# Eight 128x2048 sums of a float32 kernel, made by GpSimd instead of VectorE

## What is computed

```
x = x + W0[i015[b]] applied over the 64 rows          (L0, 64x64 per batch)
x = x + W1[i015[b]] applied over the 64 rows          (L1, 64x64 per batch)
x = x + x W^T + 0.5 (x A[i02[b]]) B^T                 (L2, W is 1024x1024, rank 32)
x = x + x W3[i37[b]]^T                                (L3, one of 8 adapters, 1024x1024)
```

## Time and profile before

| | |
|---|---|
| runs | 382.86, 383.15, 383.18 us (median 383.15) |
| profiled execution, span | 381.9 us |
| TensorE busy, 1738 matmuls | 375.4 us, 98% |
| VectorE | 267.3 us, 70% |
| ScalarE | 224.6 us, 59% |
| GpSimd | 114.9 us, 30% |
| HBM traffic over the span | 159 GB/s |

### The profile page before, as it was taken

How to read it: one execution, slowest core, us unless ns; L and a number is a source line. 1 busy time by engine, 2 the same in 40 slices (tenths; PEclk the granted TensorE clock), 3 DMA queues, 4 the chain that set the end, 5 groups by cost and what they waited for, 6 DMA issues and landing times.

```text
span 381.9 us, 7677 instructions
## 1 busy us (share of the span) xinstructions
PE 375.4 (98%) x1738; PEld 311.7 (82%) x1739; DVE 267.3 (70%) x302; ACT 224.6 (59%) x299; POOL 114.9 (30%) x156
## 2 busy tenths in 40 slices
PE   8999999999999999999999999999999999999995
PEld 5788888888888888888888888888888888888884
DVE  2796978856849888538869367854599635999653
ACT  3589568496246476235465465853677536779443
POOL 0000140100000000024765347563167532676600
PEclk9999999999999999999999999999999999999999
DMA  7985904640368484415437316652256622565223
GB/s 259 399 303 186 366 0 165 218 162 9 111 228 281 151 312 140 165 45 203 144 99 251 86 23 192 206 168 58 57 173 218 167 58 58 200 203 155 60 64 85
DMA packets 24187, 61.38 MB, mean 161 GB/s; under 512 B 1906, under 2 KB 2098, under 8 KB 24114
## 3 DMA queue, kind: packets, MB, share of 16 engines
q1 hardware_dynamic: 23648, 60.10, 47.6%
q10 hardware_dynamic: 466, 0.44, 0.4%
HBM read 52.15 MB, written 8.39 MB: 159 GB/s over the span
## 4 chain that ended last, share of the span: by engine, by line
PE 96%; DMA 2%; SPq 1%; DVE 0%; issue 0%; ACT 0%
PE ps L1526 45%; PE ps L1382 12%; PE ps L1383 12%; PE ps L1384 12%; PE ps L1409 4%; PE ps L1552 4%; PE ps L1618 2%; PE ps L1421 2%; DMA ring_f<-wt 2%; PE ps L1448 2%; PE ps L1567 0%; PE ps L1458 0%; SPq L315 0%; PE ps L1651 0%; DVE ring L906 0%; SPq L321 0%
## 5 line engine op out<-in xcount | busy, mean ns | idle before, releaser
L1526 PE MATMUL ps<-ring,aT 128*128 x752 | 173.2, 389 | 0.0
L1526 PEld LDWEIGHTS ps<-ring,aT 128*128 128x128 f32 x752 | 141.1, 188 | 29.6 <-issue 0.3
L1382 PE MATMUL ps<-ring 128*128 128x512 f32 x208 | 81.1, 390 | 0.0
L1383 PE MATMUL ps<-ring 128*128 128x512 f32 x208 | 81.0, 389 | 0.0
L1384 PE MATMUL ps<-ring 128*128 128x512 f32 x208 | 80.9, 389 | 0.0
L481 POOL TENSOR_TENSOR aT<-xT,aT 128x512 fp32r<-128x512 f32 (+1 forms) x36 | 56.2, 1581 | 47.4 <-ACT aT L766 42.4
L1273 DVE TENSOR_TENSOR ring<-raw,ring 128x1024 f32 (+1 forms) x40 | 61.7, 1600 | 6.2 <-ACT ring L752 6.2
L772 ACT ACTIVATE aT<-ps 64x1024 fp32r<-64x1024 f32 x32 | 32.7, 1023 | 47.5 <-PE ps L1526 47.1
L1301 DVE TENSOR_TENSOR stage<-ps,stage 64x1024 f32<-64x1024 f32 x30 | 36.7, 1222 | 28.9 <-ACT stage L781 28.2
L1290 DVE TENSOR_TENSOR aT<-ps,aT 64x1024 fp32r<-64x1024 f32 x32 | 39.1, 1222 | 21.5 <-ACT aT L772 20.8
L1382 PEld LDWEIGHTS ps<-ring 128*128 128x128 f32 x208 | 39.1, 188 | 8.1
(11 more groups left out here) (98 smaller groups left out, 326.9 us busy)
## 6 DMA issues: line engine op xcount, KB each, us to landing
raw<-w3t SPq DMA_DIRECT2D x40, 512.0 KB, 4.4
ring_f<-xt SPq DMA_DIRECT2D x8, 1024.0 KB, 8.7
raw<-xt SPq DMA_DIRECT2D x8, 1024.0 KB, 5.3
out<-stage SPq DMA_DIRECT2D x30, 256.0 KB, 3.2
ring_f<-wt SPq DMA_DIRECT2D x4, 1024.0 KB, 8.1
xT<-xt SPq DMA_DIRECT2D x3, 1024.0 KB, 10.4
xT<-wt SPq DMA_DIRECT2D x2, 1024.0 KB, 15.9
ring_f<-wt SPq DMA_DIRECT2D x4, 256.0 KB, 5.4
```

What stands on the lines that cost most here:

```text
L1382: pe.matmul(dst, hi_of(qw)[:, k, cs], hi_of(qx)[:, k, :], start=start and k == 0, stop=False, skip_group_check=True)
L1383: pe.matmul(dst, hi_of(qw)[:, k, cs], lo_of(qx)[:, k, :], start=False, stop=False, skip_group_check=True)
L1526: last = pe.matmul(acc(i)[:, n, :], x3_split(i, k, start, P), ring[:, bass.ds(off + (part * D + n * 512), 512)], start=(k == 0 and j == 0) ...
```

## The change

The functions t3, t2, t4 and t1 move from VectorE's program to GpSimd's, unchanged but for the engine. They leave VectorE's list at eight places. In GpSimd's list T3(0) and T2(0) stand ahead of the S3 diagonals, T4(0) between the S3 and the A22 diagonals, and the other five behind the A22 diagonals. Three of them get a wait for VectorE's low parts (semaphore x_lo), which its own order gave before: T3(1) for x0 to x5, T2(1) for x0 to x6, T4(1) for x0 to x8.

```diff
--- before.py
+++ after.py
@@ -519,10 +519,55 @@
+            def t3(j):
+                pool.wait_ge(s("keep"), 16 * (j + 1))
+                pool.wait_ge(s("stg"), in_stg(f"B12_{j}"))
+                pool.tensor_tensor(keep, keep, stg, ALU.subtract).then_inc(s("T3"), 1)
+            def t2(j):
+                pool.wait_ge(s("T3"), j + 1)
+                if j == 0:
+                    pool.wait_ge(s("b11"), 16)
+                else:
+                    pool.wait_ge(s("stg"), in_stg("B11_1"))
+                pool.tensor_tensor(stg, stg if j else b11, keep, ALU.add).then_inc(s("T2"), 1)
+            def t4(j):
+                n = 6 + 3 * j
+                pool.wait_ge(s(f"x_in{n}"), 16)
+                pool.wait_ge(s("T2"), j + 1)
+                v = raw_of(x_slot(n))
+                pool.tensor_tensor(v, v, stg, ALU.subtract).then_inc(s("T4"), 1)
+            def t1(j):
+                pool.wait_ge(s("stg"), in_stg(f"B11_{j} again"))
+                if j == 0:
+                    pool.wait_ge(s("x_in10"), 16)
+                    v = raw_of(x_slot(10))
+                else:
+                    pool.wait_ge(s("kw"), 48)
+                    v = kw
+                pool.tensor_tensor(v, v, stg, ALU.subtract).then_inc(s("T1"), 1)
+            t3(0)
+            t2(0)
             pool.wait_ge(s("S3"), 1)
             w_eyes(w2t, "S3")
+            t4(0)
             pool.wait_ge(s("w_in4"), 16)
             w_eyes(raw_of(w_slot(4)), "A22")
+            pool.wait_ge(s("x_lo"), HALF * 6)
+            t3(1)
+            pool.wait_ge(s("x_lo"), HALF * 7)
+            t2(1)
+            pool.wait_ge(s("x_lo"), HALF * 9)
+            t4(1)
+            t1(0)
+            t1(1)
...
             s3()
-            t3(0)
-            t2(0)
             low_parts(1)
...
             mix_twice()
-            t4(0)
             x_los(6)
             w_los(4, raw_of(w_slot(4)))
-            t3(1)
-            t2(1)
             x_los(7, stg)
             x_los(8, keep)
             take(6)
-            t4(1)
             x_los(9)
             s1()
-            t1(0)
...
             c22(0)
-            t1(1)
             x_los(13, kw)
```

More of the change, by code:

```diff
@@ L924, in x_los @@
                     x_lo(n, src, ks)
[L926 to L958, removed]
             def s2():
```

## The result

The changed kernel takes 391.44 us (389.48 to 391.87, four executions) against 383.11 (382.86 to 383.18): ratio 1.021, 95% interval 1.0185 to 1.0235. It is slower, as forecast, but by 8.3 us and not by 4.3, and the time is above the range.

A forecast was written before the change was run, and what follows sets the result against it. TensorE's unbroken matmuls bound the kernel, so relieving VectorE gains nothing. New waits of 1.6 and 2.7 us sum to 4.3; with the 383.15 us median that gives 387.4, range 385.0 to 390.2 us.

The forecast's parts named there:

- What bounds the kernel: From 18 to 182 us TensorE's matmuls run without a break, so taking work off VectorE gains 0.
- One sum, 4.5 us: One 128x2048 sum on GpSimd takes 4.5 us, against 2.29 on VectorE; at most 5.1.
- Not slower: Rival: with sums below 3.6 us all is hidden and the time is 383.2 us; chance 8%.
- The turns: GpSimd and two-SBUF-input VectorE operations alternate, so a VectorE operation meeting a sum can lose up to 4.5 us.
- Only the chain: Rival: low_lows and T3(1) meet no waits, leaving 2.1 to 2.7 us at P6(1); 385.2 to 385.9 us; chance 15%.
- Step 1: T3(0) and T2(0): low_lows wait behind T2(0), so TensorE waits 1.6 us at C11(1)'s first delta.
- Step 2: Chain of sums and loads from T4(0) to x7: x7's half reaches P6(1) 2.7 us late.
- Where it would be waited for: Of the 2.7 us, some 2.4 at C21(0) for w4's second half and 0.3 at P6(1).
- The clock: TensorE's granted clock falling below 1.00 behind a wait: named as a sign of being wrong, given no size.
- Step 3: T4(1), T1(0) and T1(1) cost 0, with cover down to a few tenths of a us.

The follow-up runs named there:

- e4: The changed kernel with only T4(1), T1(0) and T1(1) on GpSimd, the other five sums back on VectorE; 382.95 us.
- e6: e1 and e2 together: six sums on GpSimd, T2(0) behind the low_lows, T3(1) and T2(1) on VectorE; 382.97 us.
- e1: The changed kernel with one added wait: T2(0) on GpSimd starts only when both low_lows of chunk 1 are done; 386.96 us.
- e10: e5 with 27 small extra matmuls on TensorE, meant to fill its wait at P6(1); 389.32 us.
- e3: The changed kernel with 30 small extra matmuls on TensorE ahead of P6(1), inside the wait; 389.97 us.
- e9: e1 with T4(0), T3(1), T2(1) and the loads between them in halves, plan steps as in e5, T3(1) behind w4's low parts; 384.97 us.
- e7: The changed kernel with T3(1) alone back on VectorE, behind w4's low parts; 386.80 us.
- e11: The changed kernel with 14 small extra matmuls on TensorE ahead of P6(1), to fill part of the wait; 391.95 us.
- e5: e1 with two portions of VectorE's plan steps moved from ahead of x6's low parts to behind x8's; 390.58 us.
- e2: The changed kernel with T3(1) and T2(1) back on VectorE, the other six sums on GpSimd; 385.51 us.

## Why the prediction was wrong

**What bounds the kernel**: right. e4 and e6 took 3 and 6 sums off VectorE and gained nothing.

**One sum, 4.5 us**: nearly right, 4.58 to 4.61 where nothing is met. The slope between the two widths held. *Not slower*, which needed under 3.6, falls.

**The turns**: right, for small operations too (5.10 us for low_lows, undone by e1), and too narrow. I read them as a matter of two SBUF inputs, but in e10 VectorE's two copies, which have one SBUF input, took 5.33 us together beside T4(0), in place of 0.87. *Only the chain* falls with it.

**Step 1, 1.6 us**: the wait was 1.5, and 0.3 came with it for the restart, which I had no term for.

**Step 2, 2.7 us**: this term was mis-sized. The wait was 3.8. From x6's landing to P6(1) I counted 26.7 us (70.5 to 97.2); it took 27.7 (71.8 to 99.5), against about 23.9 allowed. Of the 1.0, 0.2 is in the sums (4.6 each, while the 0.1 allowed for a turn in T4(0) wasn't used), 0.3 in T3(1)'s turn (5.52, so 0.9 in place of 0.6), and 0.5 in the hops between landing, sum, ScalarE, VectorE and TensorE, some 0.1 to 0.2 each, most of which I had left out.

**Where it would be waited for**: wrong for this kernel, right for e1. I had T3(1) between w4's halves; it came some 0.2 us after the second half had begun and waited for its end (82.64), as T4(0) began at 71.86, 0.15 us after the copies behind VectorE's plan steps had ended, and the A22 diagonals met nearly nothing. I had taken this as mere bookkeeping, "these are not added". It wasn't: behind one idle time of 3.8 us the clock fell, and behind two of 2.0 and 0.5 in e1's profiled execution it didn't.

**The clock**: the step that failed most. I named a fall of the clock only as something that would make me wrong, and gave it no price and no chance: in the sum 1.6 + 2.7 its term is nothing. It is 2.85 of the 8.69 us in the profiled execution (e3 against the changed kernel). The one execution of the changed kernel with its clock at 1.000 took 389.48 us, which is inside the range; its waits aren't on record.

**Step 3, nothing**: right here and in e4. Its thin cover was real: e9, with the plan's steps later still, overran it by 1.0 us.

The sum again, from measured terms: 1.5 + 3.8 in waits, 0.5 for the restarts behind both and 2.85 for the clock, 8.65 of the 8.69. Against the 4.3 of the forecast, the clock is 2.85 of the difference, step 2 1.1, and the restarts 0.5. That the change is slower was right by its mechanism and not by luck; how much slower was not.

## What to carry to other kernels

An engine with nothing to do in the trace isn't free if it shares a turn with a busy one: price an operation by what it can hold up (here two operations of 0.43 us came 4.2 us late, and TensorE waited for them), and place it behind the short ones that are due. Taking work off the engine that isn't the bottleneck brought nothing, even where it cost nothing (e4, e6). Price moved work along its chain of loads and buffers from the first landing to the appointment, with every hop. And where a forecast makes TensorE idle, add the fall of its clock behind it as a term of the sum: behind the one wait of 3.8 us it was worth 2.85, and behind e1's two shorter ones nothing in the profiled execution.

## What the runs showed of the hardware

- A VectorE operation of 8 columns on 32 partitions took 4.58 us beside a GpSimd sum (e9), where one like it takes 0.2: it waited as long as a wide one would. Two copies, which have one SBUF input, took 5.33 us together in place of 0.87 (e10), while low_sum, which reads PSUM, was not held up (0.69 us). The Trainium skill (SBUF — State Buffer, § Who interferes with whom) calls the pair of ports that the two engines share an exclusive lock; these runs agree. They add that the two alternate when both have work queued: w4's halves with T3(1) between them took 6.77 us in e1, and 2.35 in the changed kernel.
- The clock fell about 2.9 us into an idle time of 3.8 (95.7 to 98.6) and stayed down until 5.9 us after work had resumed. It stayed up behind idle times of 1.5 us (e7), 1.9 (e11) and 2.0 (e1). Behind 3.4 (e5) it fell only 1.0 us after work had resumed, and was down for some 3.4. And it fell behind one of 2.1 (e11, in L3). So the length of a wait alone didn't decide it here.
- A wait of TensorE of 1.5 us cost 1.8 (e2); the first matmul behind it took 0.50 us in place of 0.39.
